# Attention and separable filters: next unit's first score blocks dealt out in the filter tail, statistics under the values, normalising in fours

## What is computed

```python
# layer 0: group norm, then linear attention in 8 heads of 64 channels
n = gn(x)                                  # 32 groups of 16 channels
A, Bm, V = Wa @ n + ba, Wb @ n + bb, Wv @ n + bv
G = einsum('bhms,bhns->bhmn', A, softmax(Bm, over all pixels))
x = x + einsum('bhmn,bhns->bhms', G, softmax(V, over channels))
# layer 1: group norm, then per image: upsample 2x, bias, leaky relu, downsample
n = gn(x)
y = up(n, 12 taps, rows and columns) + bias        # 266 x 266
y = clip(where(y >= 0, y, 0.2 * y) * sqrt(2), -256, 256)
x = x + down(y, 12 taps, rows and columns)         # 128 x 128
```

## Time and profile before

| | |
|---|---|
| median of 3 runs | 16631.77 us (16610.16 to 16636.97) |
| the profiled execution | 16617.44 us, its span 16615.7 us |
| TensorE products | 14628.5 us busy, 88% of the span |
| VectorE | 12382.1 us, 75% |
| ScalarE | 11322.1 us, 68% |
| GpSimd | 9035.6 us, 54% |
| DMA | mean 72 GB/s, 0.960 mean granted TensorE clock |

### The profile page before, as it was taken

How to read it: one execution, slowest core, us unless ns; L and a number is a source line. 1 busy time by engine, 2 the same in 40 slices (tenths; PEclk the granted TensorE clock), 3 DMA queues, 4 the chain that set the end, 5 groups by cost and what they waited for, 6 DMA issues and landing times.

```text
span 16615.7 us, 487793 instructions
## 1 busy us (share of the span) xinstructions
PE 14628.5 (88%) x156388; PEld 12544.6 (75%) x156388; DVE 12382.1 (75%) x26154; ACT 11322.1 (68%) x19746; POOL 9035.6 (54%) x13589
## 2 busy tenths in 40 slices
PE   7898888988889888898888888888888889888898
PEld 5777777777777777777777777777777777777787
DVE  6777777777777777777777777777777777777776
ACT  5676666766667666676666666666667666676676
POOL 4555555555555555555555555555555555555555
PEclk9999999999999999999999999999999999999999
DMA  3233222332222332223322233222332223322232
GB/s 82 59 81 90 72 61 60 78 90 75 62 62 75 88 79 60 62 73 88 83 61 61 69 88 85 63 59 66 88 86 62 61 64 87 89 64 60 63 86 49
DMA packets 1931549, 1199.83 MB, mean 72 GB/s; under 512 B 78724, under 2 KB 1864580, under 8 KB 1930244
## 3 DMA queue, kind: packets, MB, share of 16 engines
q1 hardware_dynamic: 1930244, 1183.65, 27.6%
HBM read 537.30 MB, written 268.44 MB: 48 GB/s over the span
## 4 chain that ended last, share of the span: by engine, by line
PE 59%; DVE 14%; issue 8%; ACT 8%; POOL 5%; DMA 3%; DVEq 1%; POOLq 1%; SPq 1%; ACTq 0%
PE ps L987 57%; ACT yb L613 4%; DVE yb L943 4%; DVE xh L913 3%; POOL yb L458 3%; PE ps L1057 2%; ACT z L597 2%; DVE t L898 1%; DVE sth L832 1%; DMA out<-xh 1%; POOL t1r L487 1%; DVE z L904 1%; DVE stc L656 1%; DMA p<-t 1%; DMA xh<-in_x 1%
## 5 line engine op out<-in xcount | busy, mean ns | idle before, releaser
L458 POOL TENSOR_SCALAR yb<-yb 128x532 f32<-128x532 f32 x4096 | 2595.8, 634 | 4108.1 <-DVE yb L943 4108.1
L987 PE MATMUL ps<-dn_t,yb 128*128 128x64 f32 (+1 forms) x32768 | 4402.1, 278 | 10.5 <-POOL yb L458 10.5
L987 PEld LDWEIGHTS ps<-dn_t,yb 128*128 128x128 f32 x32768 | 4075.4, 196 | 19.7 <-POOL yb L458 14.4
L943 DVE SCALAR_TENSOR_TENSOR yb<-yb 128x532 f32<-128x532 f32 x4096 | 3174.6, 775 | 971.1 <-ACT yb L613 949.2
L613 ACT ACTIVATE yb<-ps,bias_b 128x532 f32<-128x532 f32 x4096 | 2881.2, 703 | 884.9 <-PE ps L987 794.9
L987 PE MATMUL ps<-up,xn 128*128 128x266 f16 x12288 | 2133.7, 287 | 640.0 <-DVE t L898 371.2
L585 ACT ACTIVATE t<-ps 128x266 f16<-128x266 f32 x4096 | 1587.6, 388 | 1534.5 <-PE ps L987 1482.0
L898 DVE TENSOR_TENSOR t<-ps,t 128x266 f16<-128x266 f32 x4096 | 1735.5, 426 | 801.2 <-ACT t L585 695.0
L987 PE MATMUL ps<-up_a,t 128*128 128x138 f16 x15360 | 2049.3, 225 | 11.2 <-DMA t<-p 11.0
L441 POOL COPY xn<-xh 128x512 f32 x1024 | 1090.6, 1067 | 1775.8 <-PE ps L987 1075.2
L987 PE MATMUL ps<-up_b,t 128*128 128x138 f16 x15360 | 2045.1, 224 | 0.0
(11 more groups left out here) (151 smaller groups left out, 27187.9 us busy)
## 6 DMA issues: line engine op xcount, KB each, us to landing
xc<-in_x SPq DMA_DIRECT2D x512, 512.0 KB, 3.8
xh<-in_x SPq DMA_DIRECT2D x480, 512.0 KB, 5.0
out<-xh SPq DMA_DIRECT2D x480, 512.0 KB, 3.4
p<-t SPq DMA_DIRECT2D x960, 128.0 KB, 3.0
t<-t SPq DMA_DIRECT2D x960, 128.0 KB, 2.4
t<-p SPq DMA_DIRECT2D x960, 128.0 KB, 2.4
xh<-in_x SPq DMA_DIRECT2D x64, 256.0 KB, 2.9
out<-xh SPq DMA_DIRECT2D x64, 256.0 KB, 3.0
```

Of the source, the lines that this page charges most:

```text
L458: nc.gpsimd.tensor_scalar(v, v, CLAMP, -CLAMP, ALU.min, ALU.max).then_inc(s_yc, 1)
L943: nc.vector.scalar_tensor_tensor(v, v, SLOPE, v, ALU.mult, ALU.max).then_inc(s_lr, 1)
L987: return nc.tensor.matmul(o, l, r, start=start, stop=stop, skip_group_check=share)
```

## The change

1. **Seam.** The four first score blocks of the next unit are written out after batch 15, dealt out among its last filter steps on TensorE, VectorE and ScalarE (`attend_first`, `max_first`, `exp_first`), and the unit's loop begins with block 4. The statistics, average, variance and scaled weights for the next unit move into batch 15 (VectorE's at images 2, 4, 6, TensorE's at 3 and 5, ScalarE's sqrt at 4). ScalarE's first four gathers stand at images 1, 3, 5, 7 of batch 15; the ring xcb moves from yb to t1. The last 16 images of the next unit are loaded twice: a copy xlate (in xn_2) in batch 15, for GpSimd's gather, which becomes two copies a block, and into xh itself after the stores. The output banks of the tail change, and the last unit is written out apart from the loop.
2. **Statistics.** The bn_stats of groups 0 and 1 are taken block by block in the value stage (two of 16 images by 4 columns for each block).
3. **Fours.** Normalising is done in halves of four images; batch 1's float32 copy and low half move from VectorE to GpSimd (`first_batches`); ScalarE's steps stand at images 2 to 5 (4 to 7 in batch 0), GpSimd's low quarters one after each of images 4 to 7. In batch 0 the first up_columns precede the next batch's first up_rows.
4. **Remainder rows** are copied at image 7 of the batch before (`keep_rows`).

The diff, cut to its core:

```diff
 # SyncE
+            def load_copy(u):
+                for i in range(0, LATE, IMG):
+                    sp.dma_start(xlate[:, i:i + IMG, :], x_row[u, :, P - LATE + i:P - LATE + i + IMG, :]).then_inc(s_xa, 16)
...
+                    if not after(1) and more:
+                        load_copy(u + 1)
...
                 steps(sp, NBAT, 2, batch, 2)
-                store_last(0)
                 wait_alone(sp, s_st[0], 16 * (NBAT // 2 * (u + 1)))
                 if more:
-                    load_xh(u + 1, NBAT - 2, 0)
+                    load_before_last(u + 1)
+                store_last(0)
+                store_last(1)
 # GpSimd
-                nc.gpsimd.tensor_copy(xhb[par], xh_wc[:, bass.ts(k, WB), :]).then_inc(s_xhb, 1)
+                nc.gpsimd.tensor_copy(xhb[par][:, :, 0:P - LATE], xh_wc[:, bass.ts(k, WB), 0:P - LATE])
+                nc.gpsimd.tensor_copy(xhb[par][:, :, P - LATE:P], xlate_wc[:, bass.ts(k, WB), :]).then_inc(s_xhb, 1)
...
+            def first_batches(u):
+                g = NBAT * u + 1
+                wait_alone(pool, s_r1, GROUPS * u + 1)
+                wait_alone(pool, s_xn, 2 * g)
+                for h in range(2):
+                    c = slice(h * HALF, (h + 1) * HALF)
+                    nc.gpsimd.tensor_scalar(xn[:, c, :], xh[:, IMG + h * HALF:IMG + (h + 1) * HALF, :], nm1[:, 0, 0:1],
+                                            r1[:, 0:1], ALU.add, ALU.mult).then_inc(s_xs, 1)
+                for h in range(2):
+                    norm_low_half(g, 1, h)
+                keep_rows(NBAT * u, 0)
...
-                wait_alone(pool, s_t1, IMG * (g + 1))
-                nc.gpsimd.tensor_copy(t1r[:, par, :, :, :], t1[:, par, :, :, 2 * P:UP].rearrange("p t i q -> p t q i")).then_inc(s_tq, 1)
                 for i in range(IMG):
+                    if i == IMG - 1 and after(1):
+                        keep_rows(g + 1, 1 - par)
                     clip_image(g, i, par)
 # ScalarE
+            def exp_first(u, k):
+                exp_block(u, k, k)
+                gather_c(k + RING, k)
...
+                        now = 4 if first else LAG
+                        if i == now and after(2) and par == 0:
+                            act.wait_ge(s_r1, GROUPS * u + j // 2 + 2)
+                        if now <= i < now + 4 and after(2):
+                            if (i - now) % 2:
+                                xn_high(j + 2, par, 1, (i - now) // 2)
+                            else:
+                                norm(j + 2, 1, (i - now) // 2)
+                        if not after(1) and more:
+                            if i % 2:
+                                gather_first(u + 1, i // 2)
+                            if i == 4:
+                                sqrt0(u + 1)
...
                 remainder_high(NBAT * (u + 1) - 1, zr_ps)
-                sqrt0(u + 1)
+                if more:
+                    for k in range(RING):
+                        exp_first(u + 1, k)
 # VectorE
+                def block_stats(k):
+                    for gr, st in enumerate((stc, stg)):
+                        last = nc.vector.bn_stats(st[:, bass.ds(k, 1), :].rearrange("p a b -> p (a b)"),
+                                                  xh[:, gr * GROUP:(gr + 1) * GROUP, bass.ts(k, WB)])
+                    return last
...
                         norm_z(k - 2, par)
+                    if before(4):
+                        block_stats(k - 4)
...
-                for q in range(4):
-                    last = group_stats(0, 0, q)
-                link(last, base + 2)
-                link(nc.vector.bn_aggr(mvh[:, 0, :], sth[:, 0, :, :].rearrange("p a b -> p (a b)")), base + 3)
+                wait_alone(dve, s_st1, (GROUPS - 1) * u + 1)
+                link(nc.vector.bn_aggr(mvh[:, 0, :], stc[:].rearrange("p a b -> p (a b)")), base + 2)
...
-                        if first and i == 0:
-                            for p in range(4):
-                                last = group_stats(1, 1, p)
-                            last.then_inc(s_st1, 1)
...
+                        if more and not after(1):
+                            tail = base + N_SMALL - N_NORM0
+                            if i == 2:
+                                norm0_stats(u + 1, tail)
+                            if i == 4:
+                                norm0_variance(u + 1, tail)
+                            if i == 6:
+                                norm0_scales(u + 1, tail)
                 steps(dve, NBAT, 2, batch, 2)
...
+                if more:
+                    max_first(u + 1, 0)
+                down_low(g, 3)
+                remainder_low(g, zr_ps)
+                if more:
+                    max_first(u + 1, 1)
                 for half in range(2):
-                    add_out(NBAT * (u + 1) - 1, NBAT - 1, half, last_ps[half])
+                    add_out(g, NBAT - 1, half, last_ps[half])
+                if more:
+                    for k in range(2, RING):
+                        max_first(u + 1, k)
 # TensorE
-                pe.wait_ge(s_t1, IMG * NBAT * u + HALF)
                 steps(pe, NBAT, 2, batch, 2)
                 g = NBAT * (u + 1) - 1
+                if more:
+                    pe.wait_ge(s_w, u + 2)
+                    pe.wait_ge(s_y, IMG * (g + 1) - 1 + YCREDIT)
+                    proj_b(u + 1, 0, 0)
                 pe.wait_ge(s_z1, 4 * g + 2 + DCREDIT)
                 pe.wait_ge(s_o, 2 * g + OCREDIT)
                 down_columns(0, last_ps[0])
-                for i in range(IMG - LAG, IMG):
-                    if i == IMG - 1:
-                        norm0_average(u + 1)
-                    down_rows(g, i, 1)
+                down_rows(g, IMG - 2, 1)
+                if more:
+                    proj_b(u + 1, 1, 1)
+                down_rows(g, IMG - 1, 1)
                 pe.wait_ge(s_y, IMG * (g + 1) + YCREDIT)
+                pe.wait_ge(s_z1, 4 * g + 3 + DCREDIT)
                 remainder_columns(g, 1, zr_ps)
-                norm0_bias(u + 1)
+                if more:
+                    attend_first(u + 1, 0)
                 pe.wait_ge(s_z1, 4 * g + 4 + DCREDIT)
                 down_columns(1, last_ps[1])
                 pe.wait_ge(s_zr, g + 1 + ONE)
                 for half in range(2):
                     down_remainder(half, last_ps[half])
+                if more:
+                    pe.wait_ge(s_o, 2 * g + 1 + OCREDIT)
+                    attend_first(u + 1, 1)
+                    attend_first(u + 1, 2)
+                    pe.wait_ge(s_o, 2 * g + 2 + OCREDIT)
+                    attend_first(u + 1, 3)
...
-            with pe.Fori(0, UNITS) as u:
-                unit(u)
+            with pe.Fori(0, UNITS - 1) as u:
+                unit(u, True)
+            unit(UNITS - 1, False)
```

360 lines of the change are left out of this document (205 added, 155 removed).

## The result

The kernel after takes 16185.0 us (median of four runs, 16181.9 to 16188.8), the kernel before 16634.4 beside it: a ratio of 0.973, 95% interval 0.972 to 0.975. Predicted were 16010 us, 15700 to 16330. Of 618 us expected, 429 came between the profiled executions (449 between the medians), and 16180 was the figure of the rival by which the seam gives nothing.

The account below looks back on a forecast made before the run. TensorE was taken as the bound, or nearly, except in the seam, passage and batch 0. Seam 170, passage and batch 0 208, steady batches 240 sum to 618 us off 16617.4; adjusted to the median, about 16010, range 15700 to 16330.

Parts of the forecast that it names:

- the rival by which the seam gives nothing: Seam: the loop's stall hits three engines in turn and the clock stays low; 16180 us, chance 0.14.
- The sign that I had named as that of a wrong forecast: All windows: the waits go but the windows keep their length, or GpSimd's new work holds up the first up-rows.
- The loop's stall: Seam: ScalarE's 2.61 us of issue at the loop's end stays, overlapping on three engines; 2.6 us kept, bounds 0 and 5.2.
- The clock: Seam: half of the last 6 us of work runs at the 1.2 GHz level after the remaining gaps; 3.0 us lost.
- The rule on taken branches: Seam: a branch to an unfetched page stalls each engine; if not overlapped 5.2 us, and the seam gives 2.9 us.
- (a): Passage: 2.47 us of bn_stats leave the chain, a last pair stays, the aggregate reads more; 1.3 us earlier.
- (b): Passage: normalising in fours lets the first up-rows start 1.2 us earlier.
- (c): Passage and batch 0: TensorE's 4.59 us wait for group 1's means gets 1.7 us shorter; 1.0 taken.
- (d): Passage and batch 0: TensorE's 3.48 us wait for GpSimd's low half of batch 2 shrinks to about 1.0; 2.5 us gained.
- (e): Batches 0 and 1: the granted clock (0.85, 0.86) should rise; 1.5 us gained of 46.6.
- The rival that they give nothing: Steady batches: VectorE's own chain sets the pace and the wait only changes its name; 16250 us, chance 0.18.
- the slower rival: Value stage: the added bn_stats pairs make VectorE the bound, from 0.88 us for one instruction; slower, chance 0.03.

Follow-up runs that it names:

- the old order: Kernel after with only the seam put back: weight steps, gathers and score blocks 0 to 3 follow the filter steps, loops close as before; 16028 us.
- hint_old_order: Kernel after with the seam put back as in the old order, plus closing branches announced on TensorE, ScalarE and VectorE; 15956 us.
- hint_loops: Kernel after, with TensorE, ScalarE and VectorE announcing the unit loop's closing branch at the top of each turn; 15980 us.
- stats_back: Kernel after, with statistics of groups 0 and 1 taken as before: four bn_stats in the passage, four in batch 0, none under the values; 16180 us.
- first_whole: Kernel after, with ScalarE's two normalising steps for batch 2 whole and an image later again, GpSimd's low quarters two at a time; 16367 us.
- fours_off: Kernel after, with ScalarE's two normalising steps whole again in steady batches only; batch 0 keeps halves, remainder rows stay kept; 16129 us.
- rows_at_start: Kernel after, with GpSimd's copy of the remainder rows back at the start of each batch; 16998 us.

## Why the prediction was right in the sum and wrong in the seam

- **Seam, 5.5 us expected, nothing came.** 52.3 us were measured where 51.9 - 5.5 = 46.4 were forecast, 5.9 more. The sign that I had named as that of a wrong forecast came here: the waits for the gathers went and the stretch kept its length. Missing was a term: the weight steps stand on VectorE's queue ahead of image 7's leaky step, and TensorE waits 3.1 us for them. I had placed the weight steps in batch 15 and asked whether they make it longer, not whether they are done when block 0 wants them. The loop's stall was sized right (2.6 kept; 2.7 on TensorE, with the engines' stalls overlapping, not in turn), but it costs 4.4, because the work behind it runs at the lower clock. The chain to the first exp and the output banks took 1.4 + 0.8 = 2.2 where I had left 2.8.
- **The clock** was put at 3.0 us, and that was too small by as much as the missing wait. Over all 31 seams TensorE's products to block 3 take 19.2 us (23.0 in the long seams, 16.5 in the short), of which 15.0 is the work at the upper level (16.45 x 0.915 in the short seams): 4.2 lost, and 1.8 more between blocks 3 and 7 (10.6 for 8.8). I had also taken the work itself as 16.1, the product of two averages; it is 15.0.
- **Batch 15:** 0.1 taken, 1.4 measured, within its bound. Nearly all of it is the clock again: the products take 13.6 us for 12.3, at a granted clock of 0.94 instead of 1.00, and idle time is 1.1 for 1.0. The steps moved there aren't the reason, since in the old order, without them, it is 14.7 us at 0.94 too; what is, stays open. Missing wait 3.1, clock 1.2 + 1.8, batch 15 1.3, less 0.6 for the chain and 1.1 for the work: 5.7 of the 5.9.
- **Where I looked for the seam's gain.** The copy of the late images was to end GpSimd's wait. It isn't needed: SyncE's new order of stores and loads does it, which I had not costed at all. And I read only ScalarE's 2.61 us as the loop's price, where TensorE already began its first projection 1.3 us after the gather was done, by hint_old_order a stall of its own.
- **The rule on taken branches** (the Trainium skill, Runtime: NRT & Kernel Launch, Instruction fetch mechanics) came nearer in number, with 2.9 us for the seam if the stalls add. They overlap, so the number was near for another reason. The trace agrees that the branch stalls the engines: 79.7 / 30 = 2.7 us on TensorE and 79.4 / 30 = 2.6 on VectorE, both gone once announced in hint_loops.
- **Passage, batches 0 and 1: 6.5 us expected, 8.6 measured.** The passage gave 2.5, where (a) and (b) had 1.3 after the 1.2 that the order of image 0 was to give back; nothing was given back. By stats_back (a) is 1.7 us in the passage, and 1.2 of them are gone again by the end of batch 0. (c) came in size (1.2 for 1.0), from the new order or the halves and not from the statistics. (d) came as well, 3.48 to 1.2 where I had 2.5 less, and (e): the products of batches 0 and 1 take 44.4 us before and 42.9 after, 1.5 less. first_whole shows how (d) and (e) hang together: 6.0 us come back, 2.6 as that wait, 0.6 as other waits, 2.8 in the clock. What I hadn't counted here is 0.7 of waits for VectorE's chain in batch 0, and the rows' wait at the start of batch 2 (0.8), which I had put with the steady ones.
- **Steady batches: 0.5 expected, 0.355 measured** over batches 2 to 14, by the mechanism named: rows' wait gone, VectorE's low half late next by 0.33. In batches 4 to 12 it is 0.54; the waits for the swapped rows in batches 3 and 14, on which the prediction says nothing, took the rest. The rival that they give nothing is out. The forecast multiplied by 15 batches a unit, though 438 waits are 13.7 a unit; the account multiplies by 13, as batches 1 and 15 stand in other columns.
- **Values: nothing, as forecast**; the slower rival needed 0.88 us for a bn_stats that takes 0.22.
- **The range held** because it was wide: its far end allowed for a whole stage that gives nothing, and that is what the seam did. The forecast was 174 us too good for the seam and 93 for the steady batches, 68 too poor for the passage and batches 0 and 1, and 10 at the start and the end were not reckoned: 174 + 93 - 68 - 10 = 189, the 618 expected less the 429 found. That the time met the rival's 16180 is partly luck: its stalls "in turn" didn't come, and the other two errors nearly cancel.

## What to carry to other kernels

When work moves across a loop's closing branch, ask on which engines the branch then falls into a chain, and announce it first: it is one line an engine, and with it the kernel gained 205 us, where the interleaving brought nothing. Before moving compute to hide a load, try the order of the queue that issues it. And when steps are brought forward, check that each is done when its first reader wants it: a hole of 3 us in front of TensorE can cost twice, once as idle time and once in the clock of what follows (up to 5.7 us here).

## What the runs showed of the hardware

- One closing branch cost TensorE 2.7 and VectorE 2.6 us; announced at the top of the turn, TensorE's left 2.5 us in the whole execution instead of 79.7. ScalarE's cost 76.3 / 30 = 2.5 in the old order and stayed when announced. GpSimd has a like gap, 106.4 / 31 = 3.4 us, once for each of its 31 closing branches; it was never announced, so there the branch is inferred.
- The same instructions ran to block 3 in 22 or in 28 us, and what decided which wasn't found: 0 of 31 long seams in one kernel (fours_off), 31 of 31 in another (rows_at_start), with the same code from the last up-columns on. In the kernel after the 13 long seams hold 13 x 5.7 = 74 us, so a comparison of two edits by total time alone can be off by that.
- Halving ScalarE's normalising step isn't free: the groups by shape show 803 ns for 512 elements against 1232 for 1024, where I took 0.62 from a plain copy. It was hidden.
